# Attention: the negated row maxima turned, split and spread once per half unit instead of once per unit

## What is computed

```python
q_c = q - q.mean(axis=-1, keepdims=True)
k_c = k - k.mean(axis=-1, keepdims=True)
cov = einsum('bhqd,bhkd->bhqk', q_c, k_c) / d
var = einsum('bhqo,bhko->bhqk', q_var, k_var) / d
attn = softmax(cov + var, axis=-1)
out = einsum('bhqk,bhkd->bhqd', attn, v)
```

## Time and profile before

| | |
|---|---|
| median of three runs | 1973.47 us |
| profiled execution: time, span | 1971.24 us, 1969.5 us |
| PE busy, share of the span | 1324.6 us, 67% |
| DVE busy | 1517.7 us, 77% |
| ACT busy | 918.3 us, 47% |
| attention, prologue | 93.2 to 142.3 us |
| attention, 512 steps | 142.3 to 836 us |
| its three sorts of matmul (L590, L605, L625) | 417.9, 407.2 and 313.4 us busy |

### The profile page before, as it was taken

How to read it: one execution, slowest core, us unless ns; L and a number is a source line. 1 busy time by engine, 2 the same in 40 slices (tenths; PEclk the granted TensorE clock), 3 DMA queues, 4 the chain that set the end, 5 groups by cost and what they waited for, 6 DMA issues and landing times. The chain is left out here.

```text
span 1969.5 us, 42398 instructions
## 1 busy us (share of the span) xinstructions
PE 1324.6 (67%) x15088; PEld 718.6 (36%) x15088; DVE 1517.7 (77%) x2925; ACT 918.3 (47%) x2025; POOL 253.8 (13%) x298
## 2 busy tenths in 40 slices
PE   4689999999999999941999580000000188822998
PEld 2215555554555555340666250000000033421665
DVE  5698999899989998071665676999999799971665
ACT  4508888888888888950443560002222100030443
POOL 6000000000000000025045000000000000034044
PEclk9859999999999999975999675555555599965999
DMA  3611111111111100032243229311212100012243
GB/s 90 175 42 27 32 30 30 30 30 30 42 45 30 30 3 3 2 111 58 53 68 50 79 104 161 111 43 43 57 46 60 54 0 0 0 52 58 56 67 44
DMA packets 118652, 100.85 MB, mean 51 GB/s; under 512 B 23665, under 2 KB 100018, under 8 KB 118066
## 3 DMA queue, kind: packets, MB, share of 16 engines
q1 hardware_dynamic: 101570, 84.79, 16.8%
q0 software_dynamic: 11264, 8.92, 3.1%
q10 hardware_dynamic: 5616, 4.47, 1.4%
HBM read 55.98 MB, written 31.21 MB: 44 GB/s over the span
## 5 line engine op out<-in xcount | busy, mean ns | idle before, releaser
L727 DVE TENSOR_REDUCE att_negmax<-att_ps_max 128x1 f32<-128x1024 f32 x512 | 620.9, 1223 | 66.0 <-PE att_ps_max L590 37.3
L715 ACT ACTIVATE att_probs<-att_ps_prob 128x512 f32<-128x512 f32 x1024 | 556.3, 595 | 128.7 <-PE att_ps_prob L605 126.5
L590 PE MATMUL att_ps_max<-av_k_op,av_q_op 81*32 81x512 bf16 x4096 | 417.9, 401 | 13.2 <-PEq L104 7.2
L605 PE MATMUL att_ps_prob<-av_q_op,av_k_op 99*32 99x512 bf16 x4096 | 407.2, 382 | 2.7
L625 PE MATMUL att_ps_acc<-att_probs,att_vq 128*32 128x256 f32 x4096 | 313.4, 379 | 0.0
L1935 PE MATMUL out_ps_y<-all_bo_row,all_ones 1*128 1x128 f32 x2 | 0.8, 481 | 373.2 <-PEq L104 373.2
L590 PEld LDWEIGHTS att_ps_max<-av_k_op,av_q_op 81*32 81x32 bf16 x4096 | 111.9, 97 | 146.5 <-DVE att_negmax L727 44.9
L605 PEld LDWEIGHTS att_ps_prob<-av_q_op,av_k_op 99*32 99x32 bf16 x4096 | 108.7, 95 | 146.1 <-ACT att_probs L715 94.3
L625 PEld LDWEIGHTS att_ps_acc<-att_probs,att_vq 128*32 128x32 f32 x4096 | 130.3, 111 | 78.4 <-issue 0.5
L1154 ACT ACTIVATE moe_moe_gate<-moe_moe_ps_h 128x256 f32<-128x256 f32 x122 | 46.8, 383 | 214.4 <-PE moe_moe_ps_h L1095 201.3
L1935 PEld LDWEIGHTS out_ps_y<-all_bo_row,all_ones 1*128 1x128 f32 x2 | 0.5, 308 | 373.4 <-issue 373.4
(11 more groups left out here) (277 smaller groups left out, 2038.1 us busy)
## 6 DMA issues: line engine op xcount, KB each, us to landing
moe_moe_xin<-expert_rows SPq DMA_DIRECT2D x182, 72.0 KB
av_k_op<-terms_k SPq DMA_DIRECT2D x48, 216.0 KB
av_q_op<-terms_q SPq DMA_DIRECT2D x144, 72.0 KB
solve_dec_and_windows<-solve_Xw SPq DMA_DIRECT2D x16, 256.0 KB, 3.0
solve_dec_and_windows<-solve_k SPq DMA_DIRECT2D x16, 256.0 KB, 3.7
terms_q<-qkv_parts_q SPq DMA_DIRECT2D x8, 384.0 KB, 2.6
terms_k<-qkv_parts_k SPq DMA_DIRECT2D x8, 384.0 KB, 3.1
all_w_all<-in_f_w SPq DMA_DIRECT2D x24, 128.0 KB, 2.5
```

Source lines behind the costliest of these rows:

```text
L590: mm = pe.matmul(ps_max[c * STRIP:(c + 1) * STRIP, a % 2, k * CH:(k + 1) * CH], q_op[s][0:R_ALL, h, at:at + STRIP], k_op[s][0:R_ALL, h, k ...
L605: mm = pe.matmul(ps_prob[c * STRIP:(c + 1) * STRIP, j % 2, :], k_op[s][0:R_END, h, at:at + STRIP], q_op[s][0:R_END, h, half * CH:(half + 1 ...
L715: act.activation(probs[:, j % PROBS, :], ps_prob[:, j % 2, :], ACT.Exp).then_inc(s_exp, 1)
L727: dve.tensor_reduce(negmax[:, s % 2, a:a + 1], ps_max[:, a % 2, :], AX.X, ALU.max, negate=True).then_inc(s_maxed, 1)
```

## The change

- The maxima have one running number n over all units. In a unit, the 16 maxima of half 0 come first, then those of half 1. `w` numbers the half units, from 0 to 31.
- Maxima run 24 steps ahead (`HALF` = 16 plus `LEAD` = 8) instead of 40. The prologue has 24 steps of maxima alone, and the last 24 of the 512 steps have none.
- The chain (turn, take, split, spread) is done for each half unit: after steps 9 and 25. `negmax`, `nm_rows`, `nm_rest` and `nm_parts` have 16 columns or partitions instead of 32. The turned tile goes to `ps_acc[w % 2]`.
- ACT's copy stands ahead of the exponentials of the step right after the turn (j = 20 and j = 52, which are steps 10 and 26) instead of two steps after it.
- SP spreads each part of a half unit with four DMAs, one per head: from four partitions of `nm_parts` into 512 values (1 KB) of a row of `q_op`. That is 12 DMAs for a half unit and 24 for a unit, where there were 3.
- PE waits for the rows at the start of each half.

```diff
-        negmax = m.sb("negmax", [P, 2, STEPS])
-        nm_rows = m.sb("nm_rows", [STEPS, P])
-        nm_rest = m.sb("nm_rest", [STEPS, P])
-        nm_parts = m.sb("nm_parts", [STEPS, 2, NPART, P], BF16)
+        negmax = m.sb("negmax", [P, 2, HALF])
+        nm_rows = m.sb("nm_rows", [HALF, P])
+        nm_rest = m.sb("nm_rest", [HALF, P])
+        nm_parts = m.sb("nm_parts", [HALF, 2, NPART, P], BF16)
...
-                split_max(u)
+                if u == 0:
+                    split_max(0)
+                split_max(2 * u + 1)
+                if u < B * NQ - 1:
+                    split_max(2 * u + 2)
...
-            def max_rows(u, s):
-
-                sp.wait_ge(s_nmp, u + 1)
+            def max_rows(w):
+
+                sp.wait_ge(s_nmp, w + 1)
+                half = slice(w % 2 * CH, (w % 2 + 1) * CH)
                 for i in range(NPART):
-                    sp.dma_start(q_op[s][R_MAX + i:R_MAX + i + 1, :, :].rearrange("o g t -> o (g t)"),
-                                 nm_parts[:, s % 2, i, :]).then_inc(s_nmrow, 16)
+                    for h in range(GH):
+                        sp.dma_start(q_op[w // 2 % NQ][R_MAX + i:R_MAX + i + 1, h, half],
+                                     nm_parts[h * TB // 2:(h + 1) * TB // 2, w % 2, i, :]).then_inc(s_nmrow, 16)
...
+            for u in range(B * NQ):
+                b, s = u // NQ, u % NQ
+                max_rows(2 * u + 1)
+                if u < B * NQ - 1:
+                    max_rows(2 * u + 2)
+                if b < last_b:
+                    sp.wait_ge(s_prob, 2 * STEPS * (u + 1))
+                    load(b + 1, s)
...
-                h, qt = a // TB, a % TB
+                h, qt = a % HALF // (TB // 2), a // HALF * (TB // 2) + a % (TB // 2)
...
-                if j == 0:
-                    pe.wait_ge(s_nmrow, 16 * NPART * (u + 1))
+                if j % STEPS == 0:
+                    pe.wait_ge(s_nmrow, 16 * NPART * GH * (2 * u + half + 1))
...
                     if kt == 0:
-                        if half == 0:
-                            pe.wait_ge(s_split, u + 1)
-                        elif u:
-                            pe.wait_ge(s_norm, 2 * u)
+                        pe.wait_ge(s_split, 2 * u + half + 1)
...
+            def turn_max(w):
+                pe.wait_ge(s_maxed, HALF * (w + 1))
+                if w >= 2:
+                    pe.wait_ge(s_norm, w - 1)
+                pe.transpose(ps_acc[w % 2][0:HALF, 0:P], negmax[:, w % 2, :], g.ident[:, :]).then_inc(s_nmT, 1)
+
+            for n in range(HALF + LEAD):
+                if n == HALF:
+                    turn_max(0)
                 for k in range(2):
-                    scores_for_max(0, 0, a, k)
-            turn_max(0, 0)
-            for a in range(LEAD):
-                for k in range(2):
-                    scores_for_max(0, 1, a, k)
+                    scores_for_max(n, k)
...
-                        if i == STEPS - LEAD + 1 and not (last and s == NQ - 1):
-                            turn_max(*nxt(b, s, 1))
+                        if i % HALF == HALF - LEAD + 1 and n < N_MAX + HALF - LEAD:
+                            turn_max(n // HALF - 1)
...
-            def take_max(u):
-                act.wait_ge(s_nmT, u + 1)
-                if u:
-                    act.wait_ge(s_nmp, u)
-                act.activation(nm_rows[:, :], ps_acc[0][0:STEPS, 0:P], ACT.Copy).then_inc(s_split, 1)
+            def take_max(w):
+                act.wait_ge(s_nmT, w + 1)
+                if w:
+                    act.wait_ge(s_nmp, w)
+                act.activation(nm_rows[:, :], ps_acc[w % 2][0:HALF, 0:P], ACT.Copy).then_inc(s_split, 1)
...
-                        if j == 2 * (STEPS - LEAD + 3) and not (last and s == NQ - 1):
-                            take_max(u + 1)
+                        if j % STEPS == 2 * (HALF - LEAD + 2) and not (last and s == NQ - 1 and j >= STEPS):
+                            take_max(2 * u + 1 + j // STEPS)
...
```

More of the change, by code:

```diff
@@ L462 @@
 STEPS = GH * TB
+HALF = STEPS // 2
+N_MAX = B * NQ * STEPS
 STRIP = 32
@@ L512, in prev @@
             return (b, s - 1) if s else (b - 1, NQ - 1)
-        def nxt(b, s, k):
-            return (b, s + k) if s + k < NQ else (b + 1, s + k - NQ)
         block = m.block()
@@ L522, in _, with split_max @@
             pool.wait_ge(s_clear, 1)
[L524 to L530, removed]
+            def split_max(w):
+                pool.wait_ge(s_split, w + 1)
+                if w >= 2:
+                    pool.wait_ge(s_nmrow, 16 * NPART * GH * (w - 1))
+                chain = Count(pool, s_nmch, 4 * w)
+                rows, rest, parts = nm_rows[:, :], nm_rest[:, :], nm_parts[:, w % 2]
                 chain.done(pool.tensor_copy(parts[:, 0, :], rows))
@@ L552, in load @@
                     load_terms(sp, g, scr, b, s, i)
-            def max_rows(u, s):
-                sp.wait_ge(s_nmp, u + 1)
+            def max_rows(w):
+                sp.wait_ge(s_nmp, w + 1)
+                half = slice(w % 2 * CH, (w % 2 + 1) * CH)
                 for i in range(NPART):
-                    sp.dma_start(q_op[s][R_MAX + i:R_MAX + i + 1, :, :].rearrange("o g t -> o (g t)"),
-                                 nm_parts[:, s % 2, i, :]).then_inc(s_nmrow, 16)
+                    for h in range(GH):
+                        sp.dma_start(q_op[w // 2 % NQ][R_MAX + i:R_MAX + i + 1, h, half],
+                                     nm_parts[h * TB // 2:(h + 1) * TB // 2, w % 2, i, :]).then_inc(s_nmrow, 16)
             for s in range(EARLY, NQ):
                 load(0, s)
[L563 to L573, removed]
+            max_rows(0)
+            for u in range(B * NQ):
[6 more added lines that the diff above has]
+                    load(b + 1, s)
         LOADS = 16 * (NPART + NPART * NPART)
@@ L578, in _, with scores_for_max @@
         def _(pe):
-            def scores_for_max(b, s, a, k):
-                u = NQ * b + s
+            def scores_for_max(n, k):
+                u, a = n // STEPS, n % STEPS
+                b, s = u // NQ, u % NQ
                 if k == 0:
@@ L584, in scores_for_max @@
                         pe.wait_ge(g.s_load[s], LOADS * (b + 1))
-                    if not (b == 0 and s == 0 and a < 2):
-                        pe.wait_ge(s_maxed, STEPS * u + a - 1)
-                h, qt = a // TB, a % TB
+                    if n >= 2:
+                        pe.wait_ge(s_maxed, n - 1)
+                h, qt = a % HALF // (TB // 2), a // HALF * (TB // 2) + a % (TB // 2)
                 for c in range(P // STRIP):
                     at = qt * P + c * STRIP
-                    mm = pe.matmul(ps_max[c * STRIP:(c + 1) * STRIP, a % 2, k * CH:(k + 1) * CH],
+                    mm = pe.matmul(ps_max[c * STRIP:(c + 1) * STRIP, n % 2, k * CH:(k + 1) * CH],
                                    q_op[s][0:R_ALL, h, at:at + STRIP],
@@ L637, in combine @@
                 mm.then_inc(s_comb, 1)
[L639 to L646, removed]
-                for k in range(2):
-                    scores_for_max(0, 0, a, k)
-            turn_max(0, 0)
-            for a in range(LEAD):
-                for k in range(2):
-                    scores_for_max(0, 1, a, k)
+            def turn_max(w):
+                pe.wait_ge(s_maxed, HALF * (w + 1))
+                if w >= 2:
+                    pe.wait_ge(s_norm, w - 1)
[3 more added lines that the diff above has]
+                    turn_max(0)
+                for k in range(2):
+                    scores_for_max(n, k)
             def body(b, first, last):
@@ L656, in body @@
                     for i in range(STEPS):
-                        a = i + LEAD
-                        k, a = (1, a) if a < STEPS else (2, a - STEPS)
+                        n = STEPS * (NQ * b + s) + i + HALF + LEAD
                         for half in range(2):
-                            if not (last and s + k >= NQ):
-                                scores_for_max(*nxt(b, s, k), a, half)
+                            if n < N_MAX:
+                                scores_for_max(n, half)
                             scores_for_prob(b, s, 2 * i + half)
@@ L721, in _, with reduce_max @@
         def _(dve):
[L722 to L727, removed]
+            def reduce_max(n):
+                w, a = n // HALF, n % HALF
+                dve.wait_ge(s_scored, n + 1)
+                if a == 0 and w >= 2:
+                    dve.wait_ge(s_nmT, w - 1)
+                dve.tensor_reduce(negmax[:, w % 2, a:a + 1], ps_max[:, n % 2, :], AX.X, ALU.max,
                                   negate=True).then_inc(s_maxed, 1)
@@ L739, in normalise @@
                                   ALU.mult).then_inc(s_norm, 1)
[L741 to L744, removed]
+            for n in range(HALF + LEAD):
+                reduce_max(n)
             def body(b, first, last):
```

## The result

| | before | after |
|---|---|---|
| median | 1972.95 us | 2077.93 us |
| profiled execution: time, span | 1971.24, 1969.5 us | 2077.02, 2074.9 us |
| mean granted clock over the span | 0.828 | 0.824 |

The median before is that of four runs here. The ratio is 1.0531, with a 95% interval from 1.0506 to 1.0557: slower by 105 us. The direction was forecast (0.70 for slower), the size was not: the point was 2012.8 and the range ended at 2068.

The account below looks back on a forecast made before the run. PE was taken as the bound, paying every wait in full. From the profiled 1971.24 us, -10.7 and +50 for the waits gave 2010.5, or 2012.8 us against the median; range 1962 to 2068.

Parts of the forecast that it names:

- parts 1 to 4: Shorter prologue -19.0 us, maxima in the end steps +3.0, 16 more turns +5.3, same work elsewhere nothing: -10.7 us.
- part 5: Chain of each half unit: twelve issues make PE wait 1.6 us for the rows, 31 times, +50 us.
- the price x of an issue: Spacing between SP's back-to-back row DMAs: taken as 0.47 us, the wait being 11 x - 3.6 us.
- the upper bound from the same line: Issue spacing of 0.64 us, from the kernel before's row DMAs: PE waits 3.3 us each half, +102 us.
- case D: Row DMAs priced like L558, spacing 0.56 to 0.64 us: 2066.5 us against the median, chance 0.30.
- the landing: Last of a half unit's twelve row DMAs: lands 1.9 us after its issue starts.
- Rival E: Pauses of 3.3 us at each half also halve PE's clock, losing 4 us each: another 124 us, 2190, chance 0.05.
- the three signs: Wrong in kind if PE waits at L644, ACT's copy starts over 0.4 us after the turn's start, or clock falls.
- Rival A: The twelve issues fit before the deadline, spacing at or below 0.34 us: 1962.8 up to 1967 us, chance 0.17.
- Parts 6 and 7: Prologue's chain: no wait, or 1.7 us at 0.64 us spacing; SP's queue: loads some 3 us later, free.

Follow-up runs that it names:

- experiment 1: The changed kernel with the query operand stored half-major, so 3 issues for a half unit instead of 12: 1958.7 us, ratio 0.9928 to the kernel before.
- experiment 4: The kernel before with each part's row spread by four DMAs instead of one, 12 issues for a unit: 2085.8 us, ratio 1.0572.
- experiment 2: The changed kernel with SP issuing each part once POOL has made it, the same twelve issues: 1996.9 us, ratio 1.0124 to the kernel before.
- experiment 5: The changed kernel with SP issuing parts early only for the first half of a unit: 2042.4 us, ratio 1.0353 to the kernel before.
- experiment 6: The changed kernel with parts issued early and sixteen DMAs for a half unit, four into an unread row: 2127.5 us, ratio 1.0789 to the kernel before.

## Why the prediction was right or wrong

**Bound, parts 1 to 4: right.** PE is the bound, a chain that is late is paid in full, and the shorter prologue with its costs is worth -10.7 us. In experiment 1 the attention is 11.1 us shorter.

**Two steps failed.** The profiled execution lies 66.5 us over the sum (2077.0 against 2010.5). Of these, 38 us are the price of an issue in part 5 (the waits cost 88 us, not 50), 27 us are the clock, which the sum had at nothing, and 1 us is the prologue.

**Part 5, the price x of an issue: mis-sized.** I took 0.47 us, arguing that a DMA of 4 pieces should be cheaper than one of 32. Measured is 0.62, beside the upper bound from the same line (0.64). The argument had no row behind it: 4 pieces last 0.573 us, 8 pieces 0.635, 16 in the half-major kernel 0.589, 32 before 0.591. The issue's price does not go by the pieces. The Trainium skill's rule on the number of engines ("DMA: Bandwidth & Descriptors", "Why a DMA increments its semaphore by 16 and not by 1"), which I read as a hint to the lower half of the range, says nothing of the time of an issue. The DMA queue counts 96 packets for these twelve DMAs, 4 more each than the pieces, which agrees with four engines, and still their issue costs what that of 32 pieces does. By the row nearest in kind the sum would have been case D. The queue from 244.9 to 254 us, to be held against the earlier trace rows:

```profile
q1 hardware_dynamic: 96, 0.01, 0.8%
```

**Part 5, the landing: too long.** The last of twelve starts at about 245.02 + 11 x 0.62 = 251.8 and PE goes on at 253.4: at most 1.6 us instead of the 1.9 of L558. That is most of why the wait is 2.8 us, where 11 x 0.62 - 3.6 gives 3.2 us.

**Rival E, the clock: kept out of the sum, and it came.** I gave it 0.05 and only at a pause of 3.3 us, read from a single pause. It came at half of the pauses, at 2.6 us of idleness, and each took 1.7 us, not 4, since the full clock was back 3.4 us after it fell and not after 8. A granted clock under 1.00 in the steps was one of the three signs that I named for being wrong in kind. With the measured waits and no fall the time would have been some 2051 us, inside the range; the 27 us of the clock put it above.

**Rival A** needed x at or below 0.34 and is refuted by the same row. Parts 6 and 7 held: 0.9 us in the prologue (0 to 1.7 forecast), nothing from SP's queue.

## What to carry to other kernels

Where a chain meets a deadline with 0.9 us to spare, count the DMA issues in it before anything else: each of these copies from SBUF to SBUF costs SP about 0.6 us, whether it moves 1 KB or 8 KB. So a chain that is run twice as often should not get more DMAs at each run; a layout that makes the piece contiguous keeps it at three. Price an unseen DMA by the row of the same kind, not by its size. A pause of PE of 2.25 us or more had a fall of the clock with it in most cases here, so waits on PE don't add up linearly.

## What the runs showed of the hardware

- SBUF to SBUF issues on SP last 0.573 us for 4 pieces of 256 bytes, 0.635 for 8, 0.589 for 16 and 0.591 for 32 (medians of L563 after, L559 in experiment 4, L564 in experiment 1 and L558 before).
- Equal pauses of PE (2.63 us) may or may not have a fall to half clock with them. Of the pauses of 0.9 to 2.0 us in experiment 2 none of 30 had one, its single pause of 2.25 us had; of those of 2.6 to 2.9 us 15 of 30 after and 13 of 15 in experiment 5; of those of 3.3 us and more in experiment 6 30 of 31; of those of 4.9 us and more in experiment 4 15 of 15. Such a kernel can vary by 29 us from one execution to the next, where the change itself varies by 7.
- A second transpose right behind the first costs 0.10 to 0.12 us, where the first costs 0.33.
